# A graph network's edge pass on Trainium2: one product of 150 columns per pair of destinations, three-pair units in a ring of four PSUM banks, and stores issued by ScalarE

## The chip, the cores and the metric

The kernel runs on one core of one Trainium2 chip. The metric is the device time of one execution in microseconds; smaller is better. Times of a profile are counted from the first instruction of its span.

## The reference, cut to what matters

The reference applies four graph layers to 3125 nodes of 128 features with 103,125 directed edges sorted by destination. Each layer is preceded by a layer norm and a ReLU. The first layer makes a message per edge and sums the messages at the destination; the last one uses a weighted adjacency:

```python
msg_input = jnp.concatenate([x[src], x[dst], edge_attr], axis=-1)     # layer 0
h = jax.nn.relu(msg_input @ W1.T + b1)
messages = h @ W2.T + b2
agg = jax.ops.segment_sum(messages, dst, num_segments=x.shape[0])
...
norm = dinv[src] * w * dinv[dst]                                      # layer 3
out = jax.ops.segment_sum(h[src] * norm[:, None], dst, num_segments=n)
```

The kernel turns the sums over edges of the later layers into dense products, and for that it needs two matrices: how often each source is joined to each destination (the counts), and the sum of the edge weights for each such pair (the weights).

## The kernel before

There are three stages. `prepare` lays the edge records out; `edge_pass` runs over all edges, and makes the first layer's sums and both matrices; the later layers are dense products. The change lies in `edge_pass` alone.

The edge pass is one program per engine, written out by hand as a loop over a step number `s` from 0 to 210. It knows two kinds of work. A **group** `g` (there are `MG` = 202) is 512 edges: GpSimd gathers their source rows (`gather`, L983, four indirect DMAs into one of five slots), TensorE adds edge, band and source parts in PSUM (`build`, L1271 and L1276), ScalarE applies the ReLU and rounds to f16 (`relu`, L1197), VectorE makes the rest of that rounding (`low_parts`, L1029), TensorE sums the messages per destination (`sum_up`, L1301), and VectorE adds them to the running sums (`add`, L1040). A **round** `r` (there are `J` = 196) is 16 destinations, taken as `PAIRS` = 8 pairs, and makes the 400 columns of both matrices that belong to them (`NKEY` = 16 x 25). VectorE writes one-hot matrices (`pair_hots`, L1016 to L1022): `hot_lo` (128 sources by 128 edges) is the stationary operand, and `hot_key` holds three blocks of 50 columns: the ones, the high part of the weight, the low part of the weight. TensorE (`multiply`) makes 16 products per round: for each pair, 100 columns (ones and high parts, L1287) and 50 columns (low parts, L1289) which are added in PSUM to the high parts. A round fills two banks, and two rounds take banks 2 and 3 or 4 and 5 by turns, so `multiply(r)` waits on `adj_out` for round r-2. ScalarE (`matrix_out`) reads a round with three instructions of 400 columns: counts as fp8 (L1203), a check that no count is too large (L1207, with a sum), and weights as f32 into `aw_out`, which has three buffers (L1210). SyncE stores that buffer to `dram_aw` (`store_weights`, L916), and `matrix_out(r)` waits for the store of round r-3.

Within a step, the engines take their work in this order:

- TensorE: `build(s)`, `multiply(s)`, `sum_up(s-1)`.
- VectorE: `hots(s+1)`, `pair_hots(s+1)`, `low_parts(s)`, `add(s-1)`; every fourth step `ea_low`; and parts of a finished tile's update (`update`, `residual`, `normalise`, `low_of_tile`; 25 tiles).
- ScalarE: `relu(s)`, `matrix_out(s-1)`; every fourth step `ea_high`.
- SyncE: at every fourth step s = 4q the loads of later groups: `load_sides` (L903), `load_bands` (L911), `load_edges` (L888), and `load_rel` (L893), which waits on `hot_t` for `hots` of group 4q+3; then in every step `store_weights(s-2)`. Loads and stores of tiles stand between them. The queue is served in order.

In the rows, `arena` is the one large buffer in which nearly all tiles of this pass lie, `psum` is all eight banks, and "remote" and "issue" are ends of waits that the profile can't name more closely.

## Time and profile before

| | us |
|---|---|
| median of 3 runs | 2182.67 (2176.24 to 2184.08) |
| the profiled execution | 2173.5 |
| its span, first to last instruction | 2171.7 |
| the edge pass in it | 126 to 1357 |

The page gives the busy share of TensorE's matmuls as 67% of the span, its weight loads 44%, VectorE 47%, ScalarE 30%, GpSimd 39%, and the mean granted clock of TensorE as 0.754 of 2.4 GHz. These are means over stages of different kinds. The chain of waits that ended last lies in the late layers, after 1488 us, so it says nothing of the edge pass; that has to be read from windows, groups and waits of its own stretch.

### The profile page before, as it was taken

To read this page: it belongs to the slowest core of one execution; us is meant where nothing else is said; L and a number is where in the kernel's file an instruction comes from. 1 tells how busy PE (TensorE), PEld (TensorE's weight loads), DVE (VectorE), ACT (ScalarE), POOL (GpSimd) and SP (SyncE) were. 2 spreads that over 40 slices of the span, in tenths; PEclk is the share of its full clock that TensorE was granted. 3 is DMA by queue.
4 is the path that set the end of the run, shared out by engine and by line. 5 is a ranking of instruction groups with operands and counts; after the bars stand their busy time and mean duration, and the time that the engine had idled before them with its cause. 6 is when DMAs were issued, how large, how long until landed. Compare 5 with 4: busy or idle time off the path is not lost. (4 is left out here: it accounts for less than half of the span.)

```text
span 2171.7 us, 31085 instructions
## 1 busy us (share of the span) xinstructions
PE 1444.7 (67%) x10698; PEld 951.5 (44%) x10698; DVE 1010.8 (47%) x2912; ACT 660.5 (30%) x1704; POOL 838.6 (39%) x877
## 2 busy tenths in 40 slices
PE   3235455555555555544555555699899999899997
PEld 3123334343343333433334343356666666455544
DVE  7745556555555555555556555431442224311101
ACT  2213344333433343333334333111343333100000
POOL 5636666666666666655666664000000000000001
PEclk8656665665555665666656666799999999899998
DMA  6543444434434444433344443103110001871770
GB/s 194 145 90 110 117 125 117 120 112 125 124 112 118 129 118 113 113 111 111 111 128 117 118 116 108 30 12 139 33 29 1 10 6 40 302 265 69 263 293 29
DMA packets 200850, 245.75 MB, mean 113 GB/s; under 512 B 36794, under 2 KB 174053, under 8 KB 200674
## 3 DMA queue, kind: packets, MB, share of 16 engines
q1 hardware_dynamic: 171202, 177.71, 25.6%
q0 software_dynamic: 29472, 65.73, 11.3%
q8 instruction: 106, 1.74, 0.3%
q14 instruction: 70, 0.57, 0.1%
HBM read 174.00 MB, written 55.93 MB: 106 GB/s over the span
## 5 line engine op out<-in xcount | busy, mean ns | idle before, releaser
L983 POOL DMA_INDIRECT arena<-dram_PHL,src_of x786 | 760.3, 967 | 472.5 <-remote 215.0
L1287 PE MATMUL psum<-arena 128*128 128x100 f16 x1568 | 225.9, 251 | 265.2 <-issue 179.7
L1287 PEld LDWEIGHTS psum<-arena 128*128 128x128 f16 x1568 | 179.6, 131 | 398.7 <-issue 372.5
L1271 PE MATMUL psum<-arena 128*128 128x128 f16 x1612 | 191.4, 284 | 165.7 <-issue 94.6
L1197 ACT ACTIVATE arena<-psum 128x512 f16<-128x512 f32 x202 | 120.4, 596 | 592.3 <-remote 439.5
L1289 PE MATMUL psum<-arena 128*128 128x50 f16 x1568 | 216.4, 232 | 77.2 <-issue 76.7
L1271 PEld LDWEIGHTS psum<-arena 128*128 128x128 f16 x1612 | 144.6, 129 | 188.0 <-issue 184.9
L1040 DVE SCALAR_TENSOR_TENSOR agg_all<-psum,agg_all 128x64 f32<-128x64 f32 x202 | 44.5, 220 | 379.3 <-remote 371.4
L1289 PEld LDWEIGHTS psum<-arena 128*128 128x128 f16 x1568 | 175.9, 116 | 88.3 <-issue 86.2
L1276 PE MATMUL psum<-arena 128*128 128x512 f16 x404 | 188.0, 554 | 14.0 <-issue 13.6
L2436 PE MATMUL psum<-arena,parts_b 128*128 128x512 fp8e4 (+5 forms) x875 | 171.0, 354 | 3.2 <-PEq L2858 3.2
L2399 POOL DMA_DIRECT2D parts_a<-dram_x x7 | 5.3, 752 | 420.7 <-DMA dram_x<-parts_a 395.6
L1029 DVE SCALAR_TENSOR_TENSOR arena<-psum,arena 128x512 f16<-128x512 f32 x202 | 138.0, 683 | 47.7 <-issue 40.8
L1203 ACT ACTIVATE arena<-psum 128x400 fp8e4<-128x400 f32 x196 | 98.3, 501 | 185.1 <-DMA dram_aw<-aw_out 128.6
L1301 PE MATMUL psum<-arena 128*128 128x64 f16 x1612 | 115.1, 229 | 46.8 <-DVE agg_all L1040 22.9
L2549 PE MATMUL psum<-arena,parts_a 128*128 128x512 f32 (+2 forms) x350 | 134.1, 544 | 2.4 <-ACT late_aggT L2674 2.4
L2549 PE MATMUL psum<-arena,parts_b 128*128 128x512 f32 (+2 forms) x350 | 133.0, 539 | 1.1 <-ACT late_aggT L2674 1.1
L1018 DVE TENSOR_TENSOR arena<-psum,fields 128x1024 f16<-128x1024 f16 x196 | 133.5, 681 | 0.0
L2436 PEld LDWEIGHTS psum<-arena,parts_b 128*128 128x128 f16 (+1 forms) x875 | 89.5, 104 | 75.6 <-issue 4.9
L1207 ACT ACTIVATE arena<-psum,arena 128x400 f16<-128x400 f32 x196 | 117.0, 597 | 0.0
L1301 PEld LDWEIGHTS psum<-arena 128*128 128x128 f16 x1612 | 92.5, 122 | 53.8 <-issue 50.3
L2436 PE MATMUL psum<-arena,parts_a 128*128 128x512 fp8e4 (+5 forms) x525 | 106.2, 362 | 0.0
(345 smaller groups left out, 2126.9 us busy)
## 6 DMA issues: line engine op xcount, KB each, us to landing
dram_aw<-aw_out SPq DMA_DIRECT2D x196, 200.0 KB
arena<-dram_aw SPq DMA_DIRECT2D x6, 6400.0 KB, 20.2
arena<-dram_aw SPq DMA_DIRECT2D x3, 4800.0 KB
arena<-in_ea_quads SPq DMA_DIRECT2D x51, 256.0 KB
arena<-dram_rel SPq DMA_DIRECT2D x51, 256.0 KB
arena<-arena SPq DMA_DIRECT2D x408, 32.0 KB
arena<-dram_PHL,src_of POOLq DMA_INDIRECT x806
arena<-dram_aw SPq DMA_DIRECT2D x2, 4000.0 KB, 13.3
```

Source lines behind the costliest of these rows:

```text
L983: nc.gpsimd.indirect_dma_start(gathered_p[:, slot, k, :], None, d["PHL"], bass.IndirectOffsetOnAxis(ap=src_of[:, b:b + 1], axis=0)).then_i ...
L1018: nc.vector.tensor_tensor(in_twos(hot_lo[:, u]), every_row(row_lo, PAIRS), field(A_LO, P), ALU.is_equal)
L1029: nc.vector.scalar_tensor_tensor(out=msg_lo[:, g % 2, 0:n], in0=pre_of(g), scalar=0.0, in1=msg_hi[:, g % 2, 0:n], op0=ALU.max, op1=ALU.sub ...
L1197: nc.scalar.activation(msg_hi[:, g % 2, 0:n], pre_of(g), ACT.Relu).then_inc(relued, 1)
L1207: nc.scalar.activation(over_of[:, :].rearrange("p (t a e) -> p t a e", t=NT, e=PAIR), half_of(r, 0), ACT.Relu, bias=minus_most[:, 0:1], ac ...
L1271: nc.tensor.matmul(out[:, k * P:(k + 1) * P], side[:, s, at:at + P], node_side[:, g % NAB, part * D:(part + 1) * D], start=(part == 0 and ...
L1276: done = nc.tensor.matmul(out, ident_h[:, :], gathered_p[:, g % NPG, 0:n, part * D:(part + 1) * D], start=False, stop=(part == 1))
L1287: nc.tensor.matmul(out, hot_lo[:, u, p, :], hot_key[:, u, p, 0:2].rearrange("p a k -> p (a k)"), start=True, stop=False)
L1289: done = nc.tensor.matmul(out[:, PKEY:2 * PKEY], hot_lo[:, u, p, :], hot_key[:, u, p, 2], start=False, stop=True)
L1301: done = nc.tensor.matmul(agg_of(g), msg[:, g % 2, k * P:(k + 1) * P], hot_d[:, g % 3, k, :], start=(part == 0 and k == 0), stop=(part == ...
L2436: last = nc.tensor.matmul(psum[0:width, SUM_BANK[n % 2], 0:end - first], parts.flat[:, t * parts.block + at:t * parts.block + at + width], ...
L2549: last = nc.tensor.matmul(psum[:, 0, 0:m * W], g[k][:, t, :], slab[:, slot_of(n), 0:m, t * W:(t + 1) * W], start=(t == 0), stop=(t == NT - 1))
```

## The change

TensorE makes one product of 150 columns per pair and no longer adds the low parts of the weights in PSUM: the three blocks of 50 columns lie apart. The eight pairs of a round are split into three units (three, three and two pairs), each in one bank, and the units go round a ring of four banks (2 to 5). ScalarE reads each unit with three instructions: counts, check, and the high parts of the weights. A new VectorE function, `whole_weights`, adds the low parts to `aw_out` with three instructions per round, one per unit. The store of `aw_out` moves from SyncE's queue to ScalarE's. On ScalarE `matrix_out(s-1)` and the store now stand ahead of `relu(s)`.

```diff
+UNIT = 3
+UNITS = -(-PAIRS // UNIT)
+RING = 4
...
+        def bank_of(r, j):
+            return psum[:, NPRE + (UNITS * r + j) % RING, 0:len(pairs_of(j)) * 3 * PKEY]
...
-                    if 2 <= s < J + 2:
-                        store_weights(s - 2)
...
-                        dve.wait_ge(multiplied, r - 1)
+                        dve.wait_ge(multiplied, UNITS * (r - 1))
...
+                def whole_weights(r):
+                    whole = aw_out[:, r % 3, :].rearrange("p (t n) -> p t n", t=NT)
+                    for j in range(UNITS):
+                        dve.wait_ge(halves_out, UNITS * r + j + 1)
+                        nc.vector.scalar_tensor_tensor(out=columns_of_unit(whole, j), in0=third_of(r, j, 2),
+                                                       scalar=1 / UP, in1=columns_of_unit(whole, j), op0=ALU.mult,
+                                                       op1=ALU.add).then_inc(weights_out, 1)
...
+                    if 1 <= s <= J:
+                        whole_weights(s - 1)
                     if s < MG:
                         low_parts(s)
...
+                def store_weights(r):
+                    act.wait_ge(weights_out, UNITS * (r + 1))
+                    nc.scalar.dma_start(d["aw"][r], aw_out[:, r % 3, :]).then_inc(aw_stored[r % 3], 16)
...
                 def matrix_out(r):
-                    act.wait_ge(multiplied, r + 1)
                     if r >= 3:
                         act.wait_ge(aw_stored[r % 3], 16 * (r // 3))
...
+                    for j in range(UNITS):
+                        unit = UNITS * r + j
+                        act.wait_ge(multiplied, unit + 1)
+                        nc.scalar.activation(columns_of_unit(flat_adj[:, :, r * W:(r + 1) * W], j), third_of(r, j, 0),
+                                             ACT.Copy, saturate=True)
...
                 for s in range(MG + LAST):
+                    if 1 <= s <= J:
+                        matrix_out(s - 1)
+                    if 2 <= s < J + 2:
+                        store_weights(s - 2)
                     if s < MG:
                         relu(s)
-                    if 1 <= s <= J:
-                        matrix_out(s - 1)
...
-                    if r >= 2:
-                        pe.wait_ge(adj_out, r - 1)
-                    for p in range(PAIRS):
-                        out = pair_of(r, p)
-                        nc.tensor.matmul(out, hot_lo[:, u, p, :], hot_key[:, u, p, 0:2].rearrange("p a k -> p (a k)"),
-                                         start=True, stop=False)
-                        done = nc.tensor.matmul(out[:, PKEY:2 * PKEY], hot_lo[:, u, p, :], hot_key[:, u, p, 2],
-                                                start=False, stop=True)
-                    done.then_inc(multiplied, 1)
+                    for j in range(UNITS):
+                        unit = UNITS * r + j
+                        if unit >= RING:
+                            pe.wait_ge(weights_out, unit - RING + 1)
+                        for i, p in enumerate(pairs_of(j)):
+                            thirds = bank_of(r, j).rearrange("p (q x) -> p q x", q=3)
+                            done = nc.tensor.matmul(thirds[:, :, i * PKEY:(i + 1) * PKEY], hot_lo[:, u, p, :],
+                                                    hot_key[:, u, p], start=True, stop=True)
+                        done.then_inc(multiplied, 1)
```

On SyncE, early in the edge pass, this stood in its queue from one fourth step to the next (L903 sides, L911 bands, L888 edges, L893 `rel`, L916 the stores):

```order
L903 DMA arena<-arena 32x512 x8
L911 DMA arena<-dram_QHL 64x256 x4
L888 DMA arena<-in_ea_quads 128x512
L893 DMA arena<-dram_rel 64x2048
L916 DMA dram_aw<-aw_out 128x400 x4
L903 DMA arena<-arena 32x512 x8
```

In the same place the changed kernel has (L913, L921, L898 and L903 are the same four loads):

```order
L913 DMA arena<-arena 32x512 x8
L921 DMA arena<-dram_QHL 64x256 x4
L898 DMA arena<-in_ea_quads 128x512
L903 DMA arena<-dram_rel 64x2048
L913 DMA arena<-arena 32x512 x8
```

The four stores behind `load_rel` have left the queue. On ScalarE, around a step with `ea_high` (L1186, L1189), the order before was the ReLU and then a round of three instructions:

```order
L1197 ACTIVATE arena<-psum 128x512
L1203 ACTIVATE arena<-psum 128x25x16
L1207 ACTIVATE arena<-psum,arena 128x400
L1210 ACTIVATE aw_out<-psum 128x400
L1186 ACTIVATE arena<-arena 128x512
L1189 ACTIVATE arena<-arena 128x512
```

Now the round comes first as nine instructions in three units (L1223, L1228, L1231), then the store (L1208), then the ReLU (L1215) and `ea_high` (L1200, L1203):

```order
L1223 ACTIVATE arena<-psum 128x25x6
L1228 ACTIVATE arena<-psum,arena 128x150
L1231 ACTIVATE aw_out<-psum 128x25x6
L1223 ACTIVATE arena<-psum 128x25x6
L1228 ACTIVATE arena<-psum,arena 128x150
L1231 ACTIVATE aw_out<-psum 128x25x6
L1223 ACTIVATE arena<-psum 128x25x4
L1228 ACTIVATE arena<-psum,arena 128x100
L1231 ACTIVATE aw_out<-psum 128x25x4
L1208 DMA dram_aw<-aw_out 128x400
L1215 ACTIVATE arena<-psum 128x512
L1200 ACTIVATE arena<-arena 128x512
```

The store is issued between a round's last read and the next ReLU. On VectorE a plain step of before, from `hots` (L1001, L1003) over `pair_hots` to `low_parts` and `add`, was:

```order
L1001 TENSOR_SCALAR arena<-arena 64x512
L1003 TENSOR_TENSOR arena<-psum,rel_of 128x256
L1016 TENSOR_TENSOR arena<-psum,fields 128x8x50
L1018 TENSOR_TENSOR arena<-psum,fields 128x1024
L1021 TENSOR_TENSOR arena<-arena,fields 128x8x50
L1022 TENSOR_TENSOR arena<-arena,fields 128x8x50
L1029 SCALAR_TENSOR_TENSOR arena<-psum,arena 128x512
L1040 SCALAR_TENSOR_TENSOR agg_all<-psum,agg_all 128x64
```

It now is (L1032 is `whole_weights`):

```order
L1005 TENSOR_SCALAR arena<-arena 64x512
L1007 TENSOR_TENSOR arena<-psum,rel_of 128x256
L1020 TENSOR_TENSOR arena<-psum,fields 128x8x50
L1022 TENSOR_TENSOR arena<-psum,fields 128x1024
L1025 TENSOR_TENSOR arena<-arena,fields 128x8x50
L1026 TENSOR_TENSOR arena<-arena,fields 128x8x50
L1032 SCALAR_TENSOR_TENSOR aw_out<-psum,aw_out 128x25x6 x2
L1032 SCALAR_TENSOR_TENSOR aw_out<-psum,aw_out 128x25x4
L1041 SCALAR_TENSOR_TENSOR arena<-psum,arena 128x512
L1052 SCALAR_TENSOR_TENSOR agg_all<-psum,agg_all 128x64
```

The three new instructions stand between the one-hot matrices of the next round and `low_parts`.

## Rows read from the trace of the kernel before

**Rows 1.** Windows: length, busy us per engine with counts, clock, DMA share, GB/s.

```profile
126.00:1357.00 1231.00, 659.69 (x6817) 475.21 (x6817) 699.85 (x1997) 467.28 (x1228) 760.32 (x786) 0.62 0.41 117
```

**Rows 2.** Groups by line, 126 to 1357 us: shapes, count | busy, mean ns | idle before, releasers.

```profile
L983 POOL DMA_INDIRECT arena<-dram_PHL,src_of x786 | 760.3, 967 | 472.5 <-remote 215.0 <-issue 203.5 <-PE psum L1276 54.1
L1287 PE MATMUL psum<-arena 128*128 128x100 f16 x1568 | 225.9, 251 | 265.2 <-issue 179.7 <-ACT aw_out L1210 82.1 <-DVE arena L1022 2.1
L1289 PE MATMUL psum<-arena 128*128 128x50 f16 x1568 | 216.4, 232 | 77.2 <-issue 76.7
...
L1029 DVE SCALAR_TENSOR_TENSOR arena<-psum,arena 128x512 f16<-128x512 f32 x202 | 138.0, 683 | 47.7 <-issue 40.8 <-ACT arena L1197 6.6
...
L1203 ACT ACTIVATE arena<-psum 128x400 fp8e4<-128x400 f32 x196 | 98.3, 501 | 185.1 <-DMA dram_aw<-aw_out 128.6 <-issue 56.4
...
L1040 DVE SCALAR_TENSOR_TENSOR agg_all<-psum,agg_all 128x64 f32<-128x64 f32 x202 | 44.5, 220 | 379.3 <-remote 371.4 <-issue 7.0 <-PE psum L1301 0.7
```

**Rows 3.** Waits, 126 to 1357 us: engine, line, waited for, us in total, times, longest.

```profile
ACT arena L1203 <- DMA dram_aw<-aw_out: 128.6, 34, 8.9
SPq L937 <- DVE tail_v L1114: 96.4, 12, 10.5
SPq L893 <- DVE arena L1001: 67.5, 11, 13.5
```

**Rows 4.** Timeline around one late store: start us, length us, engine, line, operation.

```profile
636.27 0.44 SPq L893 DMA_DIRECT2D arena<-dram_rel  x1
636.76 1.06 SPq L916 DMA_DIRECT2D dram_aw<-aw_out  x2
...
641.37 0.50 ACT L1203 ACTIVATE arena<-psum 128x400 fp8e4<-128x400 f32 x1 [5.09 <-DMA dram_aw<-aw_out]
...
642.34 0.50 ACT L1210 ACTIVATE aw_out<-psum 128x400 f32<-128x400 f32 x1
642.99 0.24 PE L1287 MATMUL psum<-arena 128*128 128x100 f16 x1 [4.62 <-issue]
```

**Rows 5.** Timeline of VectorE's step, 607.00 to 608.99 us.

```profile
607.00 0.22 DVE L1040 SCALAR_TENSOR_TENSOR agg_all<-psum,agg_all 128x64 f32<-128x64 f32 x1 [0.23 <-remote]
...
608.99 0.36 DVE L1022 TENSOR_TENSOR arena<-arena,fields 128x400 f16<-128x400 f16 x1
```

**Rows 6.** Timeline of TensorE: a pause, then a step from 624.68 us on.

```profile
622.11 0.25 PE L1287 MATMUL psum<-arena 128*128 128x100 f16 x1 [1.20 <-issue]
623.49 0.20 PE L1289 MATMUL psum<-arena 128*128 128x50 f16 x1 [1.13 <-issue]
...
624.68 1.04 PE L1271 MATMUL psum<-arena 128*128 128x128 f16 x8
625.51 1.06 PE L1276 MATMUL psum<-arena 128*128 128x512 f16 x2
...
626.52 0.26 PE L1287 MATMUL psum<-arena 128*128 128x100 f16 x1
626.65 0.26 PE L1287 MATMUL psum<-arena 128*128 128x100 f16 x1
...
627.40 0.60 PE L1301 MATMUL psum<-arena 128*128 128x64 f16 x8
```

**Rows 7.** Timeline of GpSimd, two gathers of one group.

```profile
639.66 0.94 POOL L983 DMA_INDIRECT arena<-dram_PHL,src_of  x1 [0.30 <-issue]
640.91 0.94 POOL L983 DMA_INDIRECT arena<-dram_PHL,src_of  x1 [0.30 <-issue]
```

**Rows 8.** Timeline of a tile's update on VectorE and small work on ScalarE.

```profile
626.77 0.15 DVE L1102 RECIPROCAL arena<-arena 128x1 f32<-128x1 f32 x1
...
628.99 0.18 DVE L1109 BATCH_NORM_AGGREGATE arena<-arena 128x2 f32<-128x6 f32 x1
...
1352.50 0.30 ACT L1232 ACTIVATE tail_v<-tail_v 128x128 f32<-128x128 f32 x1
```

**Rows 9.** One line's instructions: durations min/median/max, first and last start.

```profile
L916 SPq DMA_DIRECT2D dram_aw<-aw_out x196: 318/436/1487, 147.7 to 1343.6; - x196
```

More of the change, by code:

```diff
@@ L793, in edge_pass @@
         trash = sb("edge_trash", [P, GE], F16)
-        over = sb("count_over", [P, J], F32)
-        over_of = sb("over_of", [P, NKEY], F16)
+        over = sb("count_over", [P, UNITS * J], F32)
+        over_of = sb("over_of", [P, UNIT * PKEY], F16)
         last = sb("flag_parts", [P, 8], F32)
@@ L818, in edge_pass @@
         pre, relued, cut, summed, added = new("pre"), new("relued"), new("cut"), new("summed"), new("added")
-        multiplied, adj_out, counted = new("multiplied"), new("adj_out"), new("counted")
+        multiplied, halves_out, weights_out, counted = (new("multiplied"), new("halves_out"), new("weights_out"),
+                                                        new("counted"))
         dve_step, flagged, checked, cleared = new("edge_dve"), new("flagged"), new("checked"), new("edge_cleared")
@@ L845, in pre_of, with pairs_of, third_of, columns_of_unit @@
             return psum[:, g % NPRE, 0:blocks_of(g) * P]
-        def pair_of(r, p):
-            return psum[:, 2 + 2 * (r % 2) + p // 4, (p % 4) * P:(p % 4) * P + 2 * PKEY]
-        def half_of(r, q):
-            u = 2 + 2 * (r % 2)
-            return psum[:, u:u + 2, :].rearrange("p b (a x) -> p (b a) x", x=P)[
-                :, :, q * PKEY:(q + 1) * PKEY].rearrange("p a (e t) -> p t a e", t=NT)
+        def pairs_of(j):
+            return range(j * UNIT, min((j + 1) * UNIT, PAIRS))
+        def bank_of(r, j):
+            return psum[:, NPRE + (UNITS * r + j) % RING, 0:len(pairs_of(j)) * 3 * PKEY]
+        def third_of(r, j, q):
+            n = len(pairs_of(j)) * PKEY
+            return bank_of(r, j)[:, q * n:(q + 1) * n].rearrange("p (a t) -> p t a", t=NT)
+        def columns_of_unit(grid, j):
+            first = PAIR * pairs_of(j)[0]
+            return grid[:, :, first:first + PAIR * len(pairs_of(j))]
         def agg_of(g):
@@ L912, in load_bands @@
                             band_in[q % 2], 16)
-                def store_weights(r):
-                    sp.wait_ge(adj_out, r + 1)
-                    sp.dma_start(d["aw"][r], aw_out[:, r % 3, :]).then_inc(aw_stored[r % 3], 16)
                 def load_tail_weights():
@@ L1156, in _ @@
                 dve.wait_ge(squared, QUADS)
-                dve.wait_ge(counted, J)
+                dve.wait_ge(counted, UNITS * J)
                 step(nc.vector.reduce_sum(d["bad_sum"][:, 1:2], over[:, :], axis=AX.X))
@@ L1199, in matrix_out @@
                 def matrix_out(r):
-                    act.wait_ge(multiplied, r + 1)
                     if r >= 3:
                         act.wait_ge(aw_stored[r % 3], 16 * (r // 3))
-                    nc.scalar.activation(flat_adj[:, :, r * W:(r + 1) * W].rearrange("p t (a e) -> p t a e", e=PAIR),
-                                         half_of(r, 0), ACT.Copy, saturate=True)
-                    if r:
-                        act.wait_ge(counted, r)
-                    nc.scalar.activation(over_of[:, :].rearrange("p (t a e) -> p t a e", t=NT, e=PAIR), half_of(r, 0),
-                                         ACT.Relu, bias=minus_most[:, 0:1], accum_out=over[:, r:r + 1]
-                                         ).then_inc(counted, 1)
-                    nc.scalar.activation(aw_out[:, r % 3, :].rearrange("p (t a e) -> p t a e", t=NT, e=PAIR),
-                                         half_of(r, 1), ACT.Copy, scale=1 / UP).then_inc(adj_out, 1)
+                    for j in range(UNITS):
[3 more added lines that the diff above has]
+                                             ACT.Copy, saturate=True)
+                        if unit:
+                            act.wait_ge(counted, unit)
+                        n = len(pairs_of(j))
+                        nc.scalar.activation(over_of[:, 0:n * PKEY].rearrange("p (t a) -> p t a", t=NT),
+                                             third_of(r, j, 0), ACT.Relu, bias=minus_most[:, 0:1],
+                                             accum_out=over[:, unit:unit + 1]).then_inc(counted, 1)
+                        nc.scalar.activation(columns_of_unit(
+                            aw_out[:, r % 3, :].rearrange("p (t n) -> p t n", t=NT), j), third_of(r, j, 1), ACT.Copy,
+                            scale=1 / UP).then_inc(halves_out, 1)
                 def keep_folded():
```

## The prediction

> **What bounds the kernel now.** I read the windows first. The edge pass takes 1231 us of the 2171.7 us span, and in it no engine is full: GpSimd 760, VectorE 700, TensorE 660, ScalarE 467 us, at a mean granted clock of 0.62 [rows 1]. With 202 groups that is 6.09 us per step. The chain that ended last lies in the late layers, so it gives no answer here; I went on to the groups and the waits of this stretch, and the reader is to look there for waits, not for busy time.
>
> GpSimd has a floor. Two gathers start 1.25 us apart when nothing holds them [rows 7], so a group of four costs 5.00 us, and the 786 gathers 982 us. It nonetheless sat idle for 472.5 us [rows 2], of which 786 x 0.30 = 236 us is the gap that belongs to each gather; the other 236 us is waiting for TensorE to free a slot. So GpSimd is near the bound and not yet the bound.
>
> TensorE's own step is 3.3 us (624.68 to 628.00) [rows 6]. It waits in `multiply`, L1287: 265 us of idle time before it, 82 us of that put down to ScalarE's L1210 [rows 2]. ScalarE in turn waited 34 times, 128.6 us in all, at L1203 for the store of `aw_out` [rows 3]. One such case in full: SyncE stands at `load_rel` until 636.27, only then issues two overdue stores, ScalarE goes on at 641.37 after 5.09 us of waiting, its three instructions end at 642.84, and TensorE's `multiply` starts at 642.99 after 4.62 us [rows 4]. The store itself was not slow; it stood in SyncE's queue behind `load_rel`, which waits on VectorE's `hots` (67.5 us, up to 13.5), and behind a tile's load (96.4 us) [rows 3].
>
> **The stores leave SyncE's queue.** Removed: 128.6 us of waiting, and behind each of the 34 waits the round itself (642.84 - 641.37 = 1.47 us [rows 4]), 34 x 1.47 = 50 us, together 179 us or 0.88 per step. The bounds are 0 (all of it returns as another wait) and 254 us, if the 56.4 us in 13 gaps that L1203 shows as "issue" [rows 2] are the same thing: 185.1 + 47 x 1.47. I take 179, the part whose releaser is named. What SyncE keeps, loads for later groups, may wait as before, and the stores no longer delay the next loads.
>
> The store now costs ScalarE's queue an issue of 0.44 us per round, 1.49 at worst [rows 9]. Behind it on ScalarE stands `relu(s)`, and VectorE's `low_parts` waits for that. It has cover: `relu(s)` needs `pre(s)`, which comes 1.9 us of `build` after the last `sum_up`, while ScalarE is busy with the round before. I cost it at nothing; without that cover it is 0.44 x 196 = 86 us. The new wait of the store, for `weights_out` of round s-2, was met one step earlier. The buffer comes back two steps later, 10 us, where the late store above took 4.6 us from issue to ScalarE's start [rows 4].
>
> Beside this: the Trainium skill ("DMA: Bandwidth & Descriptors", section "Issuing engines are not separate DMA queues") says that issuing from another engine saves only the issuing sequencer's time, usually little. By that rule alone the move would bring next to nothing. The trace agrees on the transfer and disagrees on "little": what was lost is sequencer time, but of a sequencer that stood still in front of the store.
>
> **One product of 150 columns.** Pairs start 0.13 us apart [rows 6]: that is 150 columns at 1.2 GHz, the lower of the two levels, whether they come in one instruction or in two. Streaming: no gain, 8 x 0.13 = 1.04 us per round before and after. It could lie between 0.5 us less per round (if the second instruction and weight load were the cost) and 0.1 us more. What does change is the count: 1568 matmuls and as many weight loads fewer. L1289 waits for nothing in the program, yet 76.7 us of idle stand before it, released by "issue" [rows 2]; 622.11 to 623.49 is such a pause [rows 6]. L1287 must have about as much in the middle of its rounds, so pauses cost 153 us, 0.78 per round. Per instruction that halves, to 0.39; if pauses go by time it stays. I keep both ends.
>
> **ScalarE reads units.** The same 1200 columns in nine instructions. A lower bound is today's 1.47 us per round [rows 4]; the upper one takes the nearest small instruction, 128 columns in 0.30 us [rows 8], nine times: 2.7 us. I take 1.9: two large ones start 0.97 us apart for 800 columns [rows 4], so the fixed part is mostly overlapped. ScalarE's step is then 1.9 + 0.44 + 0.60 for the ReLU, about 3.2 us with the rest, under every other chain.
>
> The Trainium skill ("ScalarE: Activation LUTs", section "Rules for kernel authors") budgets about 0.3 us per ACTIVATE and 0.83 ns per element. By it the nine cost 3.7 us and ScalarE's step some 5.2 us, a rule that speaks against the split. By the same rule the old round would be 1.9 us, where the trace has 1.47, so I give it a small chance only, within the second rival.
>
> **VectorE adds the low parts.** Three instructions per round, from PSUM: between 0.22 us each (64 columns, L1040) and 0.68 (512 columns, L1029) [rows 2]; in proportion 0.31, 0.31 and 0.26 us, so 0.9, with overlap 0.7 us per round, 137 us in all (bounds 129 and 400). VectorE has 379 us idle before `add` [rows 2] to cover the work. But its place matters: `multiply(s)` takes banks of a ring of four, so unit 1 of round s needs VectorE to be done with unit 0 of round s-1, in the same step s. That was a wait for round s-2 before.
>
> **The new step.** From `add` on VectorE (607.00) to the end of `pair_hots` (609.35) is 2.35 us [rows 5]; then 0.31 for the first unit; then TensorE's units 1 and 2, five pairs, 0.65; `sum_up` 0.60 [rows 6]; handovers about 0.1. That closes the loop at the next `add`: 4.0 us. `build` (1.7 us) lies beside VectorE's 2.66. To it come the tile updates: one of their pieces takes 2.40 us (626.77 to 629.17) [rows 8], I take twice that per tile, 25 x 4.8 / 202 = 0.60; and `ea_low`, of the shape of L1029, every fourth step, 0.17. Sum 4.77. With halved pauses 5.16, with all of them 5.55. The middle is 5.35, above GpSimd's 5.00. The subtraction agrees: 6.09 - 0.88 = 5.21, less a fifth of a microsecond of pauses, plus 0.31 for the ring. So 202 x (6.09 - 5.35) = 150 us less: 2173.5 - 150 = 2023.5 for the profiled execution. The median of the runs stands 9.2 us above the profiled one, so I forecast 2033.
>
> **Rivals.**
> - *GpSimd's floor.* Pauses and tiles hide beside the gathers. For it: 236 us of its idle time are waits for slots, and five slots even out irregular steps. Against: the 4.77 us without pauses leaves it no room. 982 us plus some 23 us at the ends gives 1005 instead of 1231: 2183 - 226 = 1957.
> - *The ring gives back half.* The stall moves to `weights_out` or to a slow nine-instruction round: TensorE waits for ScalarE's three, then VectorE's one, per unit. With ScalarE at 2.7 instead of 1.9, and half of that showing, 5.35 + 0.4 = 5.75: 2183 - 69 = 2114. For it: VectorE serves in order, so any late unit stops its `low_parts` too. Against: units are read out as they come.
> - *No difference.* The stores were late only because the engines were late; then L1203's wait reappears as L1287's. 2183. Against: the case of rows 4, where ScalarE had nothing else to wait for.
> - *Slower: lockstep.* TensorE and VectorE no longer overlap across steps: each pause delays `sum_up`, that delays `add`, `hots` and `whole_weights`, and that delays `multiply`. If every pause counts in full and VectorE's new 0.7 us and the store's 0.44 lie on the loop too: 4.77 + 0.78 + 0.4 + 0.44 = 6.39, 61 us more: 2243. It decides from 6.09 us per step on, that is, once 0.74 us per step more than I reckon lies on the loop. Against: the loop above has `build` and the store beside it.
>
> **Chances.** Forecast (5.1 to 5.6 us per step, 1983 to 2084): 0.52. GpSimd's floor: 0.10. Half given back (2084 to 2170): 0.22. No difference: 0.06. Slower: 0.10. The likeliest case is 2033. The range of 8 in 10 reaches from 1965, close to the floor, to 2155, which leaves out the two last cases and a sliver of the first and third. Within 0.5% (11 us, about what a measurement of this kernel can tell from no change) I put 0.06, faster 0.84, slower 0.10.
>
> **What would show it.** Right: the edge pass ends near 1207 us; L1223, the new first read, has hardly any wait for the store; `add` on VectorE keeps some idle time, less than 379 us; GpSimd's idle time falls to some 320 us; pairs stay 0.13 us apart at the lower clock. Wrong: long waits of the first product or its weight load on `whole_weights`; SyncE's load of sides arriving late at `build`; pauses that are as long in total with half the instructions. A much higher granted clock than 0.62 in this stretch would make it faster than I say, since `build`, products and `sum_up` all shrink with it. I am wrong altogether if ScalarE still sits idle before L1223 for over 100 us with the store as releaser.

## The result, and the profile after

| kernel | median of runs | lowest to highest | profiled execution, span | granted clock, whole span; edge pass |
|---|---|---|---|---|
| before | 2182.67 us (9 runs) | 2175.52 to 2184.84 | see above | 0.754; 0.62 |
| changed | 2190.51 us (9 runs) | 2186.32 to 2195.87 | 2186.32, 2184.5 | 0.766; 0.64 |

The ratio is 1.0042, with a 95% interval of 1.0031 to 1.0054: no gain, and if anything a loss of 8 us where 150 less had been forecast. The window of the edge pass answers to [rows 1]; the last three columns are the granted clock, the DMA share and GB/s:

```profile
core 0: us, PE busy (x) PEld busy (x) DVE busy (x) ACT busy (x) POOL busy (x), PEclk, DMA share, GB/s
126.00:1369.00 1243.00, 597.94 (x5212) 444.14 (x5213) 813.89 (x2570) 622.59 (x2793) 762.51 (x786) 0.64 0.40 116
```

The last ReLU of the pass ended at 1371.6 us, not near 1207. TensorE has 1568 matmuls less and 62 us less to do, VectorE 114 and ScalarE 155 us more, and the pass is no shorter. The groups of 126 to 1369 us, which answer to [rows 2]:

```profile
L987 POOL DMA_INDIRECT arena<-dram_PHL,src_of x786 | 762.5, 970 | 490.2 <-issue 190.1 <-PE psum L1300 172.6 <-remote 127.5
L1313 PE MATMUL psum<-arena 128*128 128x150 f16 x1568 | 243.2, 300 | 637.0 <-DVE aw_out L1032 428.9 <-issue 208.1
L1032 DVE SCALAR_TENSOR_TENSOR aw_out<-psum,aw_out 128x150 f32<-128x150 f32 (+1 forms) x588 | 136.4, 287 | 0.0
```

And the waits of 126 to 1365 us (us in total, times, longest); they answer to [rows 3]:

```profile
PE psum L1313 <- DVE aw_out L1032: 428.9, 122, 9.4
DVE agg_all L1052 <- remote: 269.1, 78, 7.5
...
PE psum L1313 <- issue: 208.1, 73, 7.7
...
ACT arena L1215 <- remote: 188.2, 74, 4.0
ACT arena L1215 <- PE psum L1300: 186.0, 97, 32.2
ACT arena L1223 <- PE psum L1313: 104.8, 80, 3.7
```

The wait for the store, 128.6 us in 34 times [rows 3], is gone: L1223 no longer waits for a DMA, and the wait for TensorE's units is its longest. In its place TensorE stands still once in each of 195 rounds (122 + 73 gaps), after its first unit of three products, until VectorE has added the low parts of the round before. That looks like the ring of four at work. But VectorE is often not late from work of its own: it stood waiting before `add`, L1052, with the releaser "remote", which is to say that no instruction's recorded end fits the release. One such step, on the timeline:

```profile
610.96 0.70 DVE L1032 SCALAR_TENSOR_TENSOR aw_out<-psum,aw_out 128x150 f32<-128x150 f32 x3
611.32 0.50 PEld L1313 LDWEIGHTS psum<-arena 128*128 128x128 f16 x5 [7.04 <-DVE aw_out L1032]
611.33 0.81 PE L1313 MATMUL psum<-arena 128*128 128x150 f16 x5 [6.75 <-DVE aw_out L1032]
...
611.93 0.63 PE L1325 MATMUL psum<-arena 128*128 128x64 f16 x8
...
613.21 1.02 PE L1300 MATMUL psum<-arena 128*128 128x512 f16 x2
...
614.06 0.37 PE L1313 MATMUL psum<-arena 128*128 128x150 f16 x3
...
614.68 0.22 DVE L1052 SCALAR_TENSOR_TENSOR agg_all<-psum,agg_all 128x64 f32<-128x64 f32 x1 [2.43 <-remote]
614.79 0.60 ACT L1215 ACTIVATE arena<-psum 128x512 f16<-128x512 f32 x1 [1.42 <-PE psum L1300]
...
615.03 0.94 POOL L987 DMA_INDIRECT arena<-dram_PHL,src_of  x1 [1.37 <-PE psum L1300]
```

`sum_up` (L1325) ends at 612.56 by the record, and `add`, which needs it and nothing else that is late, starts at 614.68: 2.12 us later. The identity products (L1300), the last part of `build`, end at 614.23, and the ReLU, which waits for them, starts at 614.79; GpSimd's next gather waits for the same release and starts at 615.03. By the record the two releases should lie 1.67 us apart; `add` and the ReLU start 0.11 us apart. VectorE had been idle for 2.43 us, ScalarE for 1.42. The end of a matmul is modelled in these records, its start and the consumer's start are not.

These 0.11 us say what is late. Between `sum_up` and the release that the ReLU waits for, TensorE has `build` to do: eight products of 128 columns and two of 512. Three products of 150 columns take 0.37 us above, about a column per cycle at 1.2 GHz; by that 2048 columns would take 0.85 us even at 2.4 GHz (an estimate; the records give them 1.86). So `sum_up` was through by 613.94, at least 0.7 us before `add` was released: that much at least is a late signal, and not late work. In the profile of before there are 75 steps in which both `add` and the next ReLU had waited, and in 49 of them the ReLU starts 0.11 us after `add`; in the changed kernel 33 of 136 are closer than 0.2 us. Where the releases are prompt (e5 below) the nearest of 65 is 1.38 us.

The Trainium skill ("Perfetto Trace Analysis", section "Tensor Engine Instruction (MATMUL, LD_WEIGHTS)") says that the profiler's end of a TensorE instruction is computed and that the semaphore moves only once PSUM has acknowledged the writes. The trace agrees, and shows how far the two can lie apart: 2.12 us in the row above.

I counted this over steps 10 to 189, in those where ScalarE waited for over 0.2 us: from the recorded end of the identity products to the start of the ReLU. Before: 149 steps, 2.74 us in the mean. Changed: 157 steps, 1.83 us. The same waits were there in the profile of before, each about three times the 128.6 us that I had priced; the second I had counted as spare time of VectorE:

```profile
ACT arena L1197 <- remote: 439.5, 106, 7.2
...
DVE agg_all L1040 <- remote: 371.4, 109, 7.8
```

### The profile page after: what moved, and what is told of

It reads as the page before. It is cut to its first block and busy times, and to the rows that moved or that the text cites. A ratio compares the mean times of both kernels' runs of the same rounds, so it can differ in the third digit from the quotient of the medians.

```text
span 2184.5 us, 30105 instructions
## 1 busy us (share of the span) xinstructions
PE 1382.6 (63%) x9130; PEld 919.3 (42%) x9130; DVE 1130.5 (52%) x3500; ACT 817.2 (37%) x3272; POOL 840.7 (38%) x877
## 5 line engine op out<-in xcount | busy, mean ns | idle before, releaser
L987 POOL DMA_INDIRECT arena<-dram_PHL,src_of x786 | 762.5, 970 | 490.2 <-issue 190.1
L1313 PE MATMUL psum<-arena 128*128 128x150 f16 x1568 | 243.2, 300 | 637.0 <-DVE aw_out L1032 428.9
L1313 PEld LDWEIGHTS psum<-arena 128*128 128x128 f16 x1568 | 162.3, 129 | 786.2 <-DVE aw_out L1032 462.3
L1215 ACT ACTIVATE arena<-psum 128x512 f16<-128x512 f32 x202 | 121.3, 600 | 381.6 <-PE psum L1300 190.8
L1223 ACT ACTIVATE arena<-psum 128x150 fp8e4<-128x150 f32 (+1 forms) x588 | 169.9, 289 | 227.4 <-PE psum L1313 104.8
L1228 ACT ACTIVATE arena<-psum,arena 128x150 f16<-128x150 f32 (+1 forms) x588 | 224.9, 382 | 10.3 <-remote 7.6
L1052 DVE SCALAR_TENSOR_TENSOR agg_all<-psum,agg_all 128x64 f32<-128x64 f32 x202 | 45.1, 223 | 335.5 <-remote 269.1
L1300 PE MATMUL psum<-arena 128*128 128x512 f16 x404 | 193.3, 576 | 2.1 <-issue 2.1
L1231 ACT ACTIVATE aw_out<-psum 128x150 f32<-128x150 f32 (+1 forms) x588 | 175.9, 299 | 0.0
L1295 PEld LDWEIGHTS psum<-arena 128*128 128x128 f16 x1612 | 150.3, 135 | 40.4 <-issue 38.8
L1041 DVE SCALAR_TENSOR_TENSOR arena<-psum,arena 128x512 f16<-128x512 f32 x202 | 137.7, 682 | 46.8 <-issue 28.0
L1032 DVE SCALAR_TENSOR_TENSOR aw_out<-psum,aw_out 128x150 f32<-128x150 f32 (+1 forms) x588 | 136.4, 287 | 0.0
L1228 ACT ACTIVATION_READ_ACCUMULATOR arena<-psum,arena 128x1 f32 x588 | 129.1, 220 | 0.0
L1325 PE MATMUL psum<-arena 128*128 128x64 f16 x1612 | 114.1, 229 | 1.8 <-DVE agg_all L1052 1.8
L1325 PEld LDWEIGHTS psum<-arena 128*128 128x128 f16 x1612 | 105.1, 126 | 5.3 <-issue 2.5
```

The costliest lines, as they stand in the source:

```text
L987: nc.gpsimd.indirect_dma_start(gathered_p[:, slot, k, :], None, d["PHL"], bass.IndirectOffsetOnAxis(ap=src_of[:, b:b + 1], axis=0)).then_i ...
L1032: nc.vector.scalar_tensor_tensor(out=columns_of_unit(whole, j), in0=third_of(r, j, 2), scalar=1 / UP, in1=columns_of_unit(whole, j), op0=A ...
L1041: nc.vector.scalar_tensor_tensor(out=msg_lo[:, g % 2, 0:n], in0=pre_of(g), scalar=0.0, in1=msg_hi[:, g % 2, 0:n], op0=ALU.max, op1=ALU.sub ...
L1223: nc.scalar.activation(columns_of_unit(flat_adj[:, :, r * W:(r + 1) * W], j), third_of(r, j, 0), ACT.Copy, saturate=True)
L1228: nc.scalar.activation(over_of[:, 0:n * PKEY].rearrange("p (t a) -> p t a", t=NT), third_of(r, j, 0), ACT.Relu, bias=minus_most[:, 0:1], a ...
L1231: nc.scalar.activation(columns_of_unit(aw_out[:, r % 3, :].rearrange("p (t n) -> p t n", t=NT), j), third_of(r, j, 1), ACT.Copy, scale=1 / ...
```

## The experiments

The runs fell on several chips. The kernel before took 1949 to 1952 us on three of them and 2170 to 2183 us on two others and where the result was measured, with nothing in between. By the numbers of the chips on record one late chip was used at two times and was late at both; the rest were used once. I call them prompt and late, after what the traces show: on the first the ReLU starts 0.04 us after the recorded end of the identity products, on the others 1.8 to 3.7 us after it. Each ratio is taken against the kernel before on the same chip. "Step" is a 180th of the time from the 10th ReLU to the 190th, and "lateness" the mean of the count above, over the steps in which ScalarE waited. In e7 to e9, e12, e16 and e17, and in e3, e4 and e13, the gathered rows are wrong or stale, and in e9, e11 and e15 the low parts are missing: these runs tell only of time.

| run | chip | median us | before | ratio [95%] | step us | lateness us |
|---|---|---|---|---|---|---|
| kernel before | late | 2182.7 | | | 6.18 | 2.74 |
| changed | late | 2190.5 | 2182.7 | 1.0042 [1.0031, 1.0054] | 6.28 | 1.83 |
| e6, kernel before | late | 2179.3 | 2177.8 | 1.0001 [0.9984, 1.0019] | 6.21 | 2.90 |
| e14, store alone | late | 2171.4 | 2179.1 | 0.9969 [0.9956, 0.9981] | 6.16 | 3.35 |
| e15, no low parts | late | 2160.6 | 2179.1 | 0.9914 [0.9896, 0.9933] | 6.13 | 3.74 |
| e18, low parts first | late | 2156.7 | 2169.5 | 0.9947 [0.9932, 0.9963] | 6.11 | 3.04 |
| e16, changed, half the gathers | late | 1919.6 | 2179.1 | 0.8809 [0.8790, 0.8828] | 4.92 | 0.15 |
| e17, changed, plain DMAs | late | 1858.6 | 2169.5 | 0.8582 [0.8555, 0.8608] | 4.62 | 0.04 |
| e7, store alone, no gathers | late | 1738.5 | 2177.8 | 0.7983 [0.7967, 0.7999] | 4.02 | 0.04 |
| e8, low parts first, no gathers | late | 1831.5 | 2177.8 | 0.8415 [0.8398, 0.8431] | 4.48 | 0.04 |
| e9, no low parts, no gathers | late | 1736.6 | 2177.8 | 0.7982 [0.7952, 0.8013] | 4.01 | 0.04 |
| e5, changed kernel | prompt | 1956.9 | 1952.2 | 1.0014 [1.0002, 1.0027] | 5.05 | 0.04 |
| e1, e10, store alone | prompt | 1952.1, 1950.5 | 1949.3, 1950.0 | 1.0008 [0.9996, 1.0020], 1.0004 [0.9991, 1.0017] | 5.06 | 0.04 |
| e2, low parts first | prompt | 1948.9 | 1949.3 | 1.0001 [0.9989, 1.0013] | 5.01 | 0.04 |
| e11, no low parts | prompt | 1948.0 | 1950.0 | 0.9985 [0.9971, 0.9999] | 5.07 | 0.04 |
| e12, changed, half the gathers | prompt | 1849.4 | 1950.0 | 0.9466 [0.9441, 0.9491] | 4.59 | 0.04 |
| e3, changed, no gathers | prompt | 1845.9 | 1949.3 | 0.9474 [0.9446, 0.9502] | 4.56 | 0.04 |
| e4, e13, before, no gathers | prompt | 1905.6, 1905.9 | 1949.3, 1950.0 | 0.9782 [0.9760, 0.9804], 0.9764 [0.9728, 0.9800] | 4.85, 4.87 | 0.04 |

In all versions with 786 gathers the step on a late chip is 6.1 to 6.3 us, whatever the edit. The lateness is no fixed delay: it grows as other waits go (2.90 to 3.35 us from e6 to e14 on one chip, 3.74 without the low parts). In its effect it is like a floor of some 6.1 us per step.

**The store alone (e1, e10, e14).** Of the change only this, on the kernel before:

```diff
-                    if 2 <= s < J + 2:
-                        store_weights(s - 2)      # SyncE
+                    if 2 <= s < J + 2:
+                        store_weights(s - 2)      # ScalarE, behind matrix_out(s - 1)
```

> The kernel before with one part of the change alone: the stores of the weighted matrices are issued by ScalarE behind matrix_out(s-1) instead of by SyncE. Theory A (the stall at late stores was real, and the change lost its gain again in the ring of four): the 129 us of ScalarE's waits for the store go, and the kernel takes 2000 to 2100 us, clearly less than before. Theory B (the steps are held at about 6.1 us by something that both kernels have, the gathers and TensorE's late completions, and the store only stood where the time was anyway): ScalarE's wait for the store goes too, but the time stays within 1% of 2183 us, and the 129 us appear as longer waits for pre and summed.

> The kernel before with only its store moved to ScalarE, all gathers in it, again, for a call in which TensorE's releases come late (the kernel before then at about 2180 us). Theory (late releases take the place of the store's wait): 2183 +- 30. Rival (the late store is on the path there too): 2017 +- 40. If the releases come promptly the time is 1951 +- 3, as it was twice, and nothing is told.

The expectations of e1 and e2 name times near 2183 us, and those of e3 and e4 start from there, but all four fell on a chip on which the kernel before takes 1949 us; only their ratios tell anything. On prompt chips the moved store is worth nothing, because GpSimd's gathers set the step. The waits of e1's edge pass:

```profile
ACT arena L1195 <- PE psum L1276: 545.0, 190, 38.4
PEld psum L1276 <- DMA arena<-dram_PHL,src_of: 458.5, 179, 5.2
...
POOL arena L977 <- issue: 238.4, 782, 0.3
```

GpSimd waits for nobody here: its 782 gaps are the 0.3 us that belong to every gather. TensorE waits for the gathers 179 times and ScalarE for TensorE 190 times. On a late chip (e14) the store alone took 7.7 us off, and the wait that it removed came back under the other name. On that chip, first the kernel before (e6), then e14:

```profile
ACT arena L1197 <- remote: 509.5, 128, 7.3
...
DVE agg_all L1040 <- remote: 366.2, 113, 7.8
...
ACT arena L1203 <- DMA dram_aw<-aw_out: 105.0, 35, 7.6
```

```profile
ACT arena L1195 <- remote: 657.0, 158, 7.3
...
DVE agg_all L1034 <- remote: 397.4, 111, 7.7
```

**The low parts first (e2, e18), and left out (e11, e15).** On VectorE, in the changed kernel:

```diff
+                    if 1 <= s <= J:
+                        whole_weights(s - 1)
                     if s + 1 < MG:
                         hots(s + 1)
                     if s + 1 < J:
                         pair_hots(s + 1)
-                    if 1 <= s <= J:
-                        whole_weights(s - 1)
```

> The changed kernel, with whole_weights(s-1) moved ahead of hots(s+1) and pair_hots(s+1) on VectorE; all else as it is. In the changed kernel TensorE waits in each of 195 rounds between unit 0 and unit 1, mostly for whole_weights. Theory A: that wait (429 us before the products) shrinks to under 100 us, and the kernel falls under 2100 us. Theory B: the wait shrinks as well, but TensorE then waits in other places, and the time stays within 1.5% of 2190 us.

> The changed kernel with whole_weights of the round before ahead of the hots on VectorE, all gathers in it. Where releases come promptly: 1949 +- 4, as it was. Where they come late: theory (the late releases set the step whatever VectorE does) 2160 to 2195; rival (TensorE's stop after unit 0 is on the path, and an earlier whole_weights shortens it by 0.5 us a step) 2050 to 2110.

> The changed kernel without whole_weights, so that the stored matrices lack their low parts; all gathers in it. TensorE's first product of a unit then waits for ScalarE alone. Where releases come promptly: 1952 +- 5, by the gathers. Where they come late: theory (late releases set the step, and whole_weights only stands in their shadow) expects the time of the changed kernel less at most 0.2 us a step, 2150 to 2190; the rival (TensorE's stop after unit 0 for whole_weights is on the path, 0.5 to 1 us of each step) expects 2000 to 2090.

> The changed kernel without whole_weights (the stored matrices lack their low parts), all gathers in it, again for a call with late releases. Theory (whole_weights stands in the shadow of the late releases): 2150 to 2190. Rival (TensorE's stop after unit 0 for whole_weights is on the path): 2000 to 2090. With prompt releases: 1949 +- 3.

On prompt chips again nothing. On late chips the earlier place is 0.5% faster than the kernel before, and no additions at all 0.9%; against the changed kernel's 1.0042 that is 1.0 and 1.3%, across chips. TensorE's stop after its first unit, 637 us by the groups, is thus worth some 28 us (1.0042 to 0.9914 of 2180) and not hundreds: it stands in the shadow of the late releases. Of the versions with all of the work in them e18 has the lowest ratio on a late chip, with e14's so near that their intervals overlap, and on a prompt one it is level with the kernel before.

**Without the gathers (e3, e4, e7, e8, e9, e13).** GpSimd issues none of the 786 gathers of the pass, so the gathered rows are stale, and TensorE waits for each of the five slots once:

```diff
-                for g in range(NPG, MG):
-                    gather(g)
+                pool.wait_ge(pre, 1)
```

> The changed kernel without the 786 gathers of the edge pass after the first five groups; TensorE uses what lies in the five slots and waits for each slot once. The messages are therefore those of other edges. Theory B, that GpSimd's gathers hold TensorE's completion signals: add and relu start within 0.2 us of the end that the profile gives to sum_up and build, where they are 1.9 and 2.1 us late now, and the step falls from 6.2 us to about 4.3, 380 us less: some 1800 us. Theory A (gathers are only a floor of 5.0 us per step, and the loop through the ring sets 6.1): the late signals stay, and the time changes by less than 3%.

> The kernel before without the 786 gathers after the first five groups, as in e3. Theory B: TensorE's signals are prompt, its pauses in the middle of products vanish, and the step falls to between 4 and 5 us, unless the late stores now show in full; 1850 to 2000 us. Theory A: the step stays near 6 us, because the late stores set it, and the time changes by less than 3%.

> The kernel before with the stores on ScalarE's queue (e1), and without the gathers after the first five groups (e4), so that GpSimd's floor is gone; the messages are those of other edges. It tells how much of the difference between e4 (1906 us) and e3 (1846 us) is the moved store. Theory A (the store was the stall): 60 us less than e4 or more, 1846 us or under. Rival (the merged products, the units or the order on ScalarE bring it): within 1% of 1906 us.

> The changed kernel with whole_weights ahead of hots and pair_hots on VectorE (e2), and without the gathers after the first five groups (e3). If the wait between unit 0 and unit 1 costs the changed kernel anything once the floor is gone, this one is faster than e3: from the trace of e3 a step of 4.56 us should fall to between 4.0 and 4.3 us, 1770 to 1820 us. If VectorE's busy time is what is left, it stays within 1% of 1846 us.

> The changed kernel without whole_weights, so the weights lack their low parts, and TensorE's banks come free after ScalarE's reads; and without the gathers after the first five groups. Against e3 it takes away both VectorE's 588 instructions and the wait on them. VectorE as the bound: 0.6 to 0.7 us per round less, 125 us, 1720 us. The wait alone as the bound: the same as e8. Neither: within 1% of 1846 us.

This is where the change's own mechanics can be seen. Two waits, the first of e4 (the kernel before), the second of e3 (changed):

```profile
ACT arena L1202 <- DMA dram_aw<-aw_out: 305.8, 53, 11.8
```

```profile
PE psum L1312 <- DVE aw_out L1031: 398.0, 195, 10.0
```

With GpSimd out of the way the late store costs 305.8 us of waiting, and moving it alone brings 1905.6 to 1738.5 us, 167 us or 0.83 per step. The changed kernel has the same moved store and stands at 1845.9: 107 us, or 0.53 per step, are taken back. Without the low-part additions they are all there again (1736.6), and put first the additions still cost 95 us (1831.5 against 1736.6, one chip). So it is the additions as work, and not the ring's wait for them, that takes most of the 107 us back. Putting them first (e8) cuts that wait from 398.0 to 235.9 us and the time by only 14. VectorE is nearly full there, busy for 795.5 of 900 us in e3 and 791.8 of 882 in e8, which is what the expectation of e8 named as the other case. The two passes, and e8's wait:

```profile
130.00:1030.00 900.00, 499.34 (x5217) 370.61 (x5215) 795.51 (x2566) 616.58 (x2795) 0.00 (x0) 0.78 0.33 102
```

```profile
130.00:1012.00 882.00, 532.56 (x5214) 368.58 (x5213) 791.81 (x2565) 610.47 (x2795) 0.00 (x0) 0.79 0.34 104
```

```profile
PE psum L1312 <- DVE aw_out L1031: 235.9, 181, 8.8
```

The single products and ScalarE's nine instructions cost nothing: e9 has them and e7 has not, at 1736.6 and 1738.5. The three kernels e7 to e9 ran on a chip on which the kernel before took 2178 us, and no release in them is late: the gathers are needed for it. e13 only repeats e4, and the differences of e7 and e8 from e3 and e4 cross chips.

**The same kernels again (e5, e6).**

> The changed kernel as it is, for a comparison on the chip of this call. Where the kernel before runs at 1949 us, as in e1 to e4, the gathers of GpSimd (5.0 us per step) set its time. Theory A (ring): the changed kernel's loop of about 4.0 us plus tiles stays under that floor there, so it takes the same time within 1%. Where the kernel before runs at 2183 us, the result repeats: 2190 us.

> The kernel before as it is, to have its trace on the chip of this call. Where it takes about 1950 us: the mean step of the edge pass is GpSimd's 5.0 to 5.1 us, relu starts 0.04 us after the end that the profile gives to build, and GpSimd does not wait for slots. Where it takes about 2183 us: steps of 6.2 us, and relu on average 2 to 3 us late, as in the first trace.

The changed kernel word for word took 1956.9 us on one chip and 2190.5 on another. Its edge pass on the prompt chip, and its two waits that matter:

```profile
126.00:1139.00 1013.00, 583.80 (x5239) 424.70 (x5240) 820.09 (x2576) 613.05 (x2795) 762.11 (x786) 0.68 0.50 142
```

```profile
ACT arena L1215 <- PE psum L1300: 332.3, 160, 39.6
...
POOL arena L987 <- issue: 238.8, 783, 0.3
PE psum L1300 <- DMA arena<-dram_PHL,src_of: 235.0, 142, 6.1
```

The busy times are those of the late chip to 2.5% (TensorE 583.8 and 597.9, GpSimd 762.1 and 762.5); 230 us of standing still are gone. From its timeline, a ReLU that waited: the identity products end at 599.47 by the record and it starts at 599.50.

```profile
598.43 1.04 PE L1300 MATMUL psum<-arena 128*128 128x512 f16 x2 [6.08 <-DMA arena<-dram_PHL,src_of]
...
599.50 0.60 ACT L1215 ACTIVATE arena<-psum 128x512 f16<-128x512 f32 x1 [5.64 <-PE psum L1300]
```

**How the lateness depends on the gathers (e12, e16, e17).** Half of them, every second block, and then all of them as plain DMAs of the same 64 KB, 128 rows of 512 B one after the other, issued by GpSimd as before:

```diff
-                    for k in range(blocks_of(g)):
+                    for k in range(0, blocks_of(g), 2):
```

```diff
-                        nc.gpsimd.indirect_dma_start(
-                            gathered_p[:, slot, k, :], None, d["PHL"],
-                            bass.IndirectOffsetOnAxis(ap=src_of[:, b:b + 1], axis=0)).then_inc(gathered[slot], 16)
+                        nc.gpsimd.dma_start(gathered_p[:, slot, k, :],
+                                            d["PHL"][(b % NT) * P:(b % NT + 1) * P, :]).then_inc(gathered[slot], 16)
```

> The changed kernel with every second gather left out (393 in place of 786), so that part of the gathered rows is stale. GpSimd's floor falls from 5.0 to 2.5 us a step. Where releases come promptly: the step of the kernel without gathers, 4.56 us, so 1848 +- 10 us. Where they come late: if each gather makes its share of the delay, half of the 1.7 us a step between 6.28 and 4.56 stays, so 5.4 us a step and 2010 +- 30; if the delay comes with any gather at all, 2100 to 2190; if it comes only when GpSimd is never done, 1850 +- 20.

> The changed kernel with every second gather left out (part of the gathered rows is stale), again for a call with late releases. If each gather makes its share of the delay: 2010 +- 30. If any gather at all makes it: 2100 to 2190. If only a GpSimd that is never done makes it: 1850 +- 20. With prompt releases: 1849 +- 5, as it was.

> The changed kernel with each of its 786 indirect DMAs replaced by a plain DMA of the same 64 KB (128 rows of 512 B in a row) into the same buffer, still issued by GpSimd; the rows are then not those of the sources. This tells what makes TensorE's releases late: the bytes that arrive, or what an indirect DMA does on GpSimd and its queue. Where releases come late (the kernel before at about 2180 us): if the bytes do it, 2150 to 2200 as with the gathers; if the indirect form does it, 1835 to 1870, the time without gathers. Where they come promptly (1950 us): 1840 to 1870 if a plain issue takes GpSimd well under the 1.25 us of a gather, 1957 if it takes as long.

On the late chip half the gathers leave a fifth of the loss: the kernel is 70 us slower than on the prompt one (1919.6 and 1849.4) where the whole ones made 234 (2190.5 and 1956.9, the latter already at GpSimd's floor) and 345 against no gathers. None of my three cases for e16 was right; the loss grows faster than the number. With plain DMAs it is gone altogether. Two views of e17, its edge pass and the queue of GpSimd's DMAs between 200 and 900 us, then the same queue for the changed kernel on a late chip and on a prompt one (e5):

```profile
126.00:1040.00 914.00, 496.46 (x5233) 370.23 (x5234) 797.06 (x2569) 617.82 (x2795) 416.90 (x786) 0.78 0.53 157
```

```profile
q0 software_dynamic: 19119, 39.20, 20.5%
```

```profile
q0 software_dynamic: 14240, 29.19, 16.5%
```

```profile
q0 software_dynamic: 17594, 36.06, 20.5%
```

(queue, kind: packets, MB, share of 16 engines). In the same 700 us e17's queue carried a third more bytes in a third more packets, and no release was late; on the same chip e18, with its gathers, has a lateness of 3.04 us. So neither the bytes nor the queue delay TensorE's signals, but something that only the indirect form has: GpSimd's work on it (0.97 us an instruction against 0.53 = 416.90 / 786), or the scattered reads. GpSimd's busy share alone doesn't decide: it is 46% in e17 and 39% in e16 (375.8 of 976 us), where some releases were still late, by up to 1.12 us. Nor are the gathers' packets slower on a late chip: by share, time and number, one took 0.13 us on both kinds.

## Why the prediction was wrong, step by step

**The stores leave SyncE's queue: this is the step that failed.** "Removed: 128.6 us of waiting ... together 179 us or 0.88 per step" measured 0.04 per step on a late chip (7.7 us / 202, e14) and 0 on a prompt one. In its place the runs show late releases of TensorE on late chips, for which the sum had no term: the store's 105.0 us went, and ScalarE's wait for a late release rose from 509.5 to 657.0 (e6, e14). On prompt chips GpSimd's gathers hold the step. The mechanism as such is real: without gathers the moved store brought 0.83 per step (e4 to e7). The prediction's lower bound, "all of it returns as another wait", is what happened.

**One product of 150 columns: right on streaming, wrong on pauses.** Three products take 0.37 us (614.06 above), 0.12 each, as forecast. The pauses of L1287 and L1289 were not a price per instruction. With half the instructions they did not halve: inside the units of the changed kernel there is none, all 637.0 us stand before the second unit. And on a prompt chip the same two instructions per pair have next to none; of e1's pass:

```profile
L1287 PE MATMUL psum<-arena 128*128 128x100 f16 x1568 | 191.2, 239 | 3.5 <-DVE arena L1016 3.0 <-ACT aw_out L1208 0.5
L1289 PE MATMUL psum<-arena 128*128 128x50 f16 x1568 | 184.7, 220 | 0.0
```

So the loop's sum failed at the same place: "pauses cost 153 us, 0.78 per round ... Per instruction that halves, to 0.39" put a price on each instruction for what goes with late releases. Those come with the gathers on some chips, 1.8 to 3.7 us in the steps that wait, and held the step at 6.28 where the sum said 5.35.

**ScalarE reads units:** a round of nine instructions ran from 601.13 to 603.32 on e5's timeline, 2.2 us against 1.9, and cost nothing (e7 and e9). By the rule of the Trainium skill ("ScalarE: Activation LUTs", section "Rules for kernel authors") it would have been 3.7 us; the trace doesn't bear it out for nine short instructions in a row.

**VectorE adds the low parts:** 588 instructions, 136.4 us against 137. The wait of the ring was named and is the longest of the changed kernel. But the sum took only 0.31 per step for it and let "379 us idle before `add`" cover the work. Those 379 us were nearly all waits for late releases (371.4), no spare time. Without gathers, where VectorE is nearly full, the additions cost 0.53 per step (e7 to e3).

**The new step:** the loop itself was right in the case shown. `add` at 608.63, `sum_up` ends at 612.56 by the record: 3.93 us against 4.0, and then 2.12 us of lateness. Without gathers the whole step is 4.56 (e3) where the sum said 4.77 before pauses; as mostly VectorE's work sets it there, the loop is not tested by it.

**The rivals.** *GpSimd's floor* forecast 1957, and e5 took 1956.9 with that floor in its waits. The agreement to the digit is luck, and it is no gain: the kernel before takes 1952 us there too, by its time on the same floor, though its trace was not taken on a prompt chip. What was missed is that the floor hides every other term. *No difference* comes nearest in time on the late chip. *Slower: lockstep* got the direction: by the count of the table the step went from 6.18 to 6.28. Its reason, a delay of TensorE that goes in full through `sum_up`, `add`, `hots`, `whole_weights` and back, was only partly so: had the lateness been a fixed delay in that loop, the moved store would have shown in full. The loss of 0.4% belongs to the additions: the low parts cost some 28 us on a late chip (e15) and the store brings 8 (e14), so by these two the changed kernel should be 20 us slower; 8 were measured, across chips.

**What I should have read.** The largest waits of the pass before were ScalarE's ReLU and VectorE's `add`, 439.5 and 371.4 us, released by "remote". I took the named releaser with 128.6 us instead. A step of 6.09 us against a floor of 5.00 and a loop of 4.0 (reckoned for the changed kernel) said that a third thing of 1 to 2 us was there.

What stays open: how much of the lateness beyond those 0.7 us, and of the pauses of before, is TensorE itself standing still, since no record tells a matmul's real end; which part of the indirect form does it; and what differs between the chips. No kernel with gathers issued by another engine or with several blocks to a gather was run. No single kernel without gathers was run on chips of both kinds.

## What to carry to other kernels

Before pricing a named wait, add up the waits whose releaser is "remote" or "issue" behind TensorE: if a consumer starts more than a few hundredths of a microsecond after the matmul's recorded end, the kernel has a term that no instruction's duration shows, and removing another wait may only move time into it, as it did here. Take away the suspected floor (here GpSimd's gathers) in one experiment first, since under a floor every other edit measures as nothing. Ask of an engine's idle time what ended it before counting it as room for new work. And run a surprising kernel on another chip before explaining it.

## What the runs showed of the hardware

The same kernel took 1949 to 1952 us on three chips and 2170 to 2183 us on others, a difference of 11 to 12% that lies wholly in the edge pass (it ends at 1139 and at 1371.6 us in the changed kernel; what follows takes 816 and 813 us). It goes with signals of TensorE that arrive late and close together (`add` and the ReLU 0.11 us apart with 2048 columns of products between them). It appears beside 786 indirect DMAs. With half of them a fifth of the loss is left, and with as many plain ones nothing. Handovers from ScalarE to VectorE (the ReLU to L1041, where that one waited) took 0.10 us on both kinds, so late releases were seen of TensorE only. A gather of 128 rows costs GpSimd 0.97 us and the 0.30 us behind it everywhere, a plain DMA of the same size 0.53 us. ACTIVATEs on 150 columns take 0.29, 0.38 and 0.30 us (L1223, L1228, L1231).
